# Pair scores as 512-column matmuls, ctx_low one step later, two first transfers from ScalarE

## The chip, the cores and the metric

The kernel runs on one core of one Trainium2 chip. The metric is device microseconds of one execution. TensorE does the matmuls and its weight loads, VectorE, ScalarE and GpSimd (POOL in the profile) work element by element, and SyncE (SP) issues DMAs. The engines run side by side and wait for each other by semaphores.

## The reference

Input x is 8 batches of 1024 rows of 1024; every batch has a context of 64 rows of 1024 and a mask. All is float32.

```
s   = layernorm(x) @ ctx.T / 32, masked         # 64 scores a row
x1  = x + softmax(s) @ ctx                      # the readout
y   = layernorm(x1)
out = x1 + y @ weight.T                         # base: 1024 columns
         + sum over the top 2 of 8 experts of
           gate * (y @ lora_A.T) @ lora_B.T * 2   # rank 16 each
```

The router's logits are y @ router_w.T; the gates are their softmax over the two largest.

## The kernel before, in words

The 8192 rows are 64 tiles of 128 rows. A tile is (b, j), batch b and j from 0 to 7. To keep float32 accuracy at the rate of the type float32r, each operand is split into a high part (rounded) and a low part (what is left), and a product is two or three matmuls: for the base product hi by hi, hi by lo and lo by hi (`three`, L1086 to L1088). The high part is made on ScalarE, the low part by a subtraction on VectorE.

Every engine runs its own list of steps, one per tile, written out by hand (`step` in each block; a hardware loop runs over batches 1 to 6). There is no planner: the order in a step is the order in which an engine takes its work. The opening, which handles tiles (0,0) and (0,1) and part of the next, has a list of its own.

TensorE's step for tile j: the base product of this tile for column group 0 (388 columns; the router's logits and the low-rank product are in it), then group 1 (386); in an odd step the scores of the pair of tiles j+3 and j+4 (`pair_scores`, L1105); the readout of tile j+2 (L1150, L1151: four matmuls of 512 columns with eT as the stationary operand); group 2; and the second low-rank product (`lora_second`), whose stationary operand is hT_hi and hT_lo.

Scores are computed turned. The stationary operand is a 128x128 block of ctxT: 64 columns with the high part of the centred context and 64 with its low part. The moving operand is a chunk of x of two tiles, 256 columns, first xT_hi (L1113) and then xT_lo (L1114). The eight chunks of the contraction make 16 matmuls that add up in the left half of the bank s_ps, 128 rows by 256 columns. VectorE turns them by 32x32 blocks (`s_transposes`, L860) into sq, four DMAs of SP carry sq's four groups of 32 rows to s_raw (`s_exchange`, L416), and `softmax_scores` (L822, L826, L830) adds the high and the low part of the context and takes the maximum.

VectorE's step, in order: `softmax_split` and `e_transposes` of tile j+2; one `xT_low`; `router_top`, which waits for the logits; `router_gate` and `h_transposes`; ctx_centre in step 4, the mask in step 5; `x2_transposes` of j+1; `s_transposes` in an odd step; `add_readout` and `norm2_stats` of j+2; `hT_low`; `norm2_moments` of j+2; `ctx_low` of the next batch in step 5 (L341 within the helper of that name, 1024 elements); `x2T_low` of j+1; ctx_sum_chunks in step 3, ctxT_low in step 4; `softmax_scores` of j+3; and the three adds of the base product.

The readout hangs on a long chain: moments on VectorE, rstd (L487) and shift (L490) on POOL, xn (L599) on ScalarE, then on SP's queue four issues of `exchange` (L374, xn to xq) and four of `e_exchange` (L410, the softmax's exponentials), and eT (L580) on ScalarE. SP's step also has the store, `h_exchange` (L404), the loads of x, xT and, in step 1, of the next batch's context, and `s_exchange` at the end of an even step.

In the opening, `pair_scores` is run for (0,2) and for (0,4). ScalarE converts xT of (0,6) as soon as the matmuls of (0,4) have read xT_hi, and then makes xn of (0,3). The matmul stream of the steady loop begins with step (0,2).

Scratch tiles such as sq and s_raw lie in w_raw[0], behind the part of it that holds a tile of x.

Of the kernel before, what the change touches and what calls it, by code (L numbers as in the profile page):

```python
# [23 lines left out]
def xattn_lora_moe_kernel(  # L24
# [35 lines left out]
    Q = 4  # L60
# [44 lines left out]
    with stack:  # L105
# [34 lines left out]
        xT_hi = sb("xT_hi", [P, 2, C, P], f32r)  # L140
        xT_lo = sb("xT_lo", [P, 2, C, P], f32r)
# [50 lines left out]
        sq = w_raw[0][:, C - 2, 0:T2]  # L192
        s_raw = w_raw[0][:, C - 3, 0:T2].rearrange("p (i k c) -> p i k c", i=Q, k=2)
# [122 lines left out]
        e_loaded = sem("e_loaded")  # L316
        sq_done = sem("sq_done")
# [16 lines left out]
        def first_ctx_low(engine, i, done):  # L334
            engine.wait_ge(ctx_hi_done, 1)
            engine.tensor_tensor(half(ctx_lo, i), half(ctx_raw, i), half(ctx_hi, i).bitcast(f32),
                                 ALU.subtract).then_inc(done, 1)

# [6 lines left out]
        def _(sp):  # L345
# [66 lines left out]
            def s_exchange(tile):  # L412

                sp.wait_ge(sq_done, pairs(tile, 1, 1 - 2))
                for i in range(Q):
                    sp.dma_start(s_raw[:, i].rearrange("p k c -> p (k c)"),  # L416
                                 sq[i * QP:(i + 1) * QP, :]).then_inc(s_loaded, 16)

            def step(tile, first=False):
# [19 lines left out]
                if j % 2 == 0 and exists(after(tile, 4)):  # L439
                    s_exchange(after(tile, 4))  # L440
# [84 lines left out]
        def _(act):  # L525
# [206 lines left out]
            norm1_squares((0, 4))  # L732
            for i in range(2):
                xT_high((0, 6), i)
# [10 lines left out]
        def _(dve):  # L745
# [112 lines left out]
            def s_transposes(tile):  # L858
                dve.wait_ge(sT_done, pairs(tile, 1, 1))
                dve.transpose(sq.rearrange("p (j k c) -> p k j c", k=2, c=QP),  # L860
                              s_ps[:, 0:T2].rearrange("p (k j c) -> p k j c", k=2, c=QP)).then_inc(sq_done, 1)
# [111 lines left out]
            def step(tile):  # L973
# [7 lines left out]
                if j % 2 == 1 and exists(after(tile, 3)):  # L981
                    xT_low(after(tile, 3), 1)
                router_top(tile)
# [17 lines left out]
                if j == TPB - 3 and exists((b, TPB)):  # L1001
                    ctx_low(dve, b + 1)
# [79 lines left out]
        def _(pe):  # L1082
# [23 lines left out]
            def pair_scores(tile):  # L1106
# [5 lines left out]
                for c in range(C):  # L1112
                    pe.matmul(s_ps[:, 0:T2], ctxT[:, c, :], xT_hi[:, :, c, :], start=(c == 0), stop=False)  # L1113
# [86 lines left out]
            def step(tile):  # L1200
# [6 lines left out]
                if j % 2 == 1 and exists(after(tile, 3)):  # L1207
                    pe.wait_ge(sq_done, pairs(after(tile, 3), 1, -2))
# [36 lines left out]
            pair_scores((0, 2))  # L1245
# [98 lines left out]
```

## Time and profile before

| | |
|---|---|
| time, median of 3 runs | 1054.68 us (1054.35 to 1054.8) |
| time of the profiled execution | 1054.39 us |
| its span | 1052.3 us |
| mean granted clock of TensorE over the span | 1.00 |
| busy: TensorE matmuls | 1043.5 us, 99% |
| busy: weight loads (beside the matmuls) | 1028.7 us, 98% |
| busy: VectorE | 817.3 us, 78% |
| busy: ScalarE | 477.7 us, 45% |
| busy: GpSimd | 147.8 us, 14% |

The span is the time from the first to the last recorded instruction of the profiled execution; the time has some 2 us around it. Busy time is the union of an engine's instructions. Matmuls are pipelined: one begins before the record of the one ahead has ended, so the rate of a stream is read from start to start and not from the durations. A granted clock of 1.00 is the upper of TensorE's two levels, 2.4 GHz.

### The profile page before, as it was taken

The page shows a single profiled execution, that of the slowest core. Times are in us where ns is not written, and L with a number is a line of the kernel's source. Part 1 is how long each engine was busy: PE and PEld are TensorE (multiplying, and loading weights), DVE is VectorE, ACT ScalarE, POOL GpSimd, SP SyncE. Part 2 cuts the span into 40 slices and gives each one's busy share as a digit, 9 for nine tenths or more (in the row PEclk, how much of TensorE's full clock was granted, in tenths as well). Part 3 has the DMA queues.
Part 4 walks back from the last instruction along what each step waited for, and adds up shares of the span by engine and source line. Part 5 has one row for each costly group of instructions (what it writes and reads, how often), then busy time and mean ns, then how long its engine had stood idle before and what let it go on. Part 6 is the DMA issues. An engine that isn't in the chain of part 4 may idle for free.

```text
span 1052.3 us, 18830 instructions
## 1 busy us (share of the span) xinstructions
PE 1043.5 (99%) x6078; PEld 1028.7 (98%) x6078; DVE 817.3 (78%) x2203; ACT 477.7 (45%) x929; POOL 147.8 (14%) x278
## 2 busy tenths in 40 slices
PE   8999999999999999999999999999999999999998
PEld 7999999999999999999999999999999999999998
DVE  6987887788777887878877888778888778777663
ACT  7754544445434544444444345344444444443320
POOL 3211211111111111111111111111111111111100
PEclk9999999999999999999999999999999999999999
DMA  8555556654556555475545655455654565554431
GB/s 306 201 160 124 149 154 163 170 147 122 149 158 179 143 123 142 143 201 131 152 115 150 185 149 150 135 132 171 163 150 137 118 174 153 152 149 114 114 75 58
DMA packets 157248, 156.81 MB, mean 149 GB/s; under 512 B 95120, under 2 KB 130064, under 8 KB 157200
## 3 DMA queue, kind: packets, MB, share of 16 engines
q1 hardware_dynamic: 156336, 154.82, 53.9%
q10 hardware_dynamic: 864, 1.45, 0.4%
q8 instruction: 18, 0.29, 0.1%
q14 instruction: 30, 0.25, 0.1%
HBM read 78.74 MB, written 33.55 MB: 107 GB/s over the span
## 4 chain that ended last, share of the span: by engine, by line
PE 95%; DVE 2%; DMA 1%; POOL 0%; issue 0%; ACT 0%; SPq 0%; ACTq 0%; DVEq 0%; POOLq 0%
PE base_ps L1086 28%; PE base_ps L1088 28%; PE base_ps L1087 28%; PE ro_ps L1150 3%; PE s_ps L1114 3%; PE ro_ps L1151 3%; PE s_ps L1113 3%; DMA xT_raw<-in_xT 1%; DVE stats L885 0%; DVE w_lo L331 0%; DVE x_first L879 0%; SPq L374 0%; DVE xT_lo L801 0%; DMA w_raw<-w_raw 0%; SPq L410 0%
## 5 line engine op out<-in xcount | busy, mean ns | idle before, releaser
L1086 PE MATMUL base_ps<-w_hi,xT_hi 128*128 128x388 f32 x1512 | 513.7, 340 | 0.0
L1088 PE MATMUL base_ps<-w_hi,xT_lo 128*128 128x388 f32 x1512 | 512.5, 339 | 0.0
L1087 PE MATMUL base_ps<-w_lo,xT_hi 128*128 128x388 f32 x1512 | 511.4, 338 | 0.0
L1087 PEld LDWEIGHTS base_ps<-w_lo,xT_hi 128*128 128x128 f32 x1512 | 284.7, 188 | 2.8
L1086 PEld LDWEIGHTS base_ps<-w_hi,xT_hi 128*128 128x128 f32 x1512 | 284.0, 188 | 2.7
L1088 PEld LDWEIGHTS base_ps<-w_hi,xT_lo 128*128 128x128 f32 x1512 | 284.3, 188 | 0.0
L487 POOL TENSOR_TENSOR rstd<-var_eps,neg_half 128x1 f32<-128x1 f32 x64 | 65.3, 1020 | 567.7 <-DVE var_eps L892 567.7
L901 DVE STREAM_TRANSPOSE x2T<-xq 128x512 f32<-128x512 f32 x122 | 121.5, 1072 | 5.3 <-DMA xq<-xn 4.7
L605 ACT CAST xT_hi<-x2T 128x512 fp32r<-128x512 f32 x122 | 69.6, 618 | 85.3 <-DVE x2T L901 85.3
L916 DVE MAX8 top<-base_ps 128x8 f32<-128x8 f32 x64 | 11.2, 174 | 106.8 <-PE base_ps L1088 106.8
L599 ACT ACTIVATE xn<-w_raw,shift,rstd 128x1024 f32<-128x1024 f32 x32 | 39.9, 1245 | 94.1 <-POOL shift L490 94.1
L908 DVE TENSOR_TENSOR xT_lo<-x2T,xT_hi 128x512 fp32r<-128x512 f32 x122 | 78.3, 683 | 0.0
L599 ACT ACTIVATE xn<-x_first,shift,rstd 128x1024 f32<-128x1024 f32 x29 | 36.1, 1245 | 82.7 <-POOL shift L490 82.7
L801 DVE TENSOR_TENSOR xT_lo<-xT_raw,xT_hi 128x1024 fp32r<-128x1024 f32 x62 | 73.4, 1185 | 0.0
L580 ACT CAST eT<-w_raw 128x128 fp32r<-128x128 f32 x60 | 17.9, 298 | 113.1 <-DMA w_raw<-w_raw 113.1
L609 ACT ACTIVATE gate_num<-top 128x1 f32<-128x1 f32 x64 | 18.9, 296 | 101.7 <-DVE top L916 101.7
L563 ACT CAST xT_hi<-xT_raw 128x1024 fp32r<-128x1024 f32 x64 | 63.9, 1045 | 1.5 <-PE s_ps L1114 1.4
L1086 PE MATMUL base_ps<-b_hi,hT_hi 128*128 128x386 f32 (+1 forms) x192 | 61.5, 320 | 0.0
L1088 PE MATMUL base_ps<-b_hi,hT_lo 128*128 128x386 f32 (+1 forms) x192 | 61.0, 318 | 0.0
L1087 PE MATMUL base_ps<-b_lo,hT_hi 128*128 128x386 f32 (+1 forms) x192 | 60.9, 317 | 0.0
L1114 PE MATMUL s_ps<-xT_lo,ctxT 128*128 128x256 f32 x248 | 60.6, 283 | 0.0
L1113 PE MATMUL s_ps<-xT_hi,ctxT 128*128 128x256 f32 x248 | 60.3, 279 | 0.0
(128 smaller groups left out, 1382.5 us busy)
## 6 DMA issues: line engine op xcount, KB each, us to landing
xT_raw<-in_xT SPq DMA_DIRECT2D x62, 512.0 KB, 5.3
xq<-xn SPq DMA_DIRECT2D x244, 128.0 KB, 3.6
w_raw<-in_x SPq DMA_DIRECT2D x32, 512.0 KB, 3.5
out<-x_first SPq DMA_DIRECT2D x32, 512.0 KB, 2.7
out<-w_raw SPq DMA_DIRECT2D x31, 512.0 KB, 2.7
x_first<-in_x SPq DMA_DIRECT2D x30, 512.0 KB, 3.5
h<-w_raw SPq DMA_DIRECT2D x248, 16.0 KB, 1.9
w_raw<-w_raw SPq DMA_DIRECT2D x120, 32.0 KB, 1.9
```

Of the source, the lines that this page charges most:

```text
L487: pool.tensor_tensor(rstd2[:, :], var_eps2[:, :], neg_half[:, :], ALU.pow).then_inc(rstd2_done, 1)
L563: act.copy(xT_hi[:, i], xT_raw[:, k, i]).then_inc(xT_hi_done, 1)
L599: act.activation(xn[:, :], x(tile), ACT.Identity, bias=shift2[:, :], scale=rstd2[:, :]).then_inc(xn_done, 1)
L605: act.copy(chunks(xT2_hi[:, tile[1] % 2], i), chunks(x2T, i)).then_inc(x2T_hi_done, 1)
L801: dve.tensor_tensor(xT_lo[:, i], xT_raw[:, tile[1] // 2 % 2, i], xT_hi[:, i].bitcast(f32), ALU.subtract).then_inc(xT_split, 1)
L901: dve.transpose(out_[:, i * QS:(i + 1) * QS], xq[:, i * QS:(i + 1) * QS, :].rearrange("p g (c n) -> p g c n", n=QP)).then_inc(x2T_done, 1)
L908: dve.tensor_tensor(chunks(xT2_lo[:, k], i), chunks(x2T, i), chunks(xT2_hi[:, k], i).bitcast(f32), ALU.subtract).then_inc(x2T_split, 1)
L1086: pe.matmul(out_, a_hi, w_h, start=start, stop=False, skip_group_check=again)
L1087: pe.matmul(out_, a_hi, w_l, start=False, stop=False, skip_group_check=again)
L1088: return pe.matmul(out_, a_lo, w_h, start=False, stop=stop, skip_group_check=again)
L1113: pe.matmul(s_ps[:, 0:T2], ctxT[:, c, :], xT_hi[:, :, c, :], start=(c == 0), stop=False)
L1114: mm = pe.matmul(s_ps[:, 0:T2], ctxT[:, c, :], xT_lo[:, :, c, :], start=False, stop=(c == C - 1))
```

## The change

The scores of a pair are computed by 8 matmuls of 512 columns, in place of 16 of 256. xT_hi and xT_lo become the two halves of one tile, xT_parts, so that a moving operand can take a chunk of both; the products with the high and the low part of x land in the left and the right half of s_ps. VectorE adds the halves (`tensor_reduce` into s_sum, in PSUM the two terms lie 256 columns apart) and then transposes s_sum, behind a semaphore of its own. TensorE's wait before the next pair is for that sum instead of for the transposes. The pair (0,2) keeps the old form under the name first_pair_scores.

ctx_low of the next batch moves from step 5, between the moments and x2T_low, to step 6, in front of router_top. Of the four transfers of the scores of the pair (0,4), the first two are issued by ScalarE, between the squares of (0,4) and the conversion of xT of (0,6); it waits there for sq_done.

```diff
--- before.py
+++ after.py
@@ -137,8 +137,9 @@
         xn = sb("xn", [P, D])
         xq = sb("xq", [P, Q, DQ])
         xT_raw = sb("xT_raw", [P, 2, 2, C, P])
-        xT_hi = sb("xT_hi", [P, 2, C, P], f32r)
-        xT_lo = sb("xT_lo", [P, 2, C, P], f32r)
+        xT_parts = sb("xT_parts", [P, 2, 2, C, P], f32r)
+        xT_hi = xT_parts[:, 0]
+        xT_lo = xT_parts[:, 1]
         sT = sb("sT", [P, T2])
         x2T = sb("x2T", [P, C, P])
         xT2_hi = sb("xT2_hi", [P, 2, C, P], f32r)
@@ -190,6 +191,7 @@
         eq = w_raw[0][:, C - 1, P:2 * P]
         e_raw = w_raw[0][:, C - 1, 2 * P:3 * P]
         sq = w_raw[0][:, C - 2, 0:T2]
+        s_sum = w_raw[0][:, C - 4, 0:T2]
         s_raw = w_raw[0][:, C - 3, 0:T2].rearrange("p (i k c) -> p i k c", i=Q, k=2)
 
 
@@ -314,6 +316,7 @@
         hq_done = sem("hq_done")
         eq_done = sem("eq_done")
         e_loaded = sem("e_loaded")
+        s_sum_done = sem("s_sum_done")
         sq_done = sem("sq_done")
         s_loaded = sem("s_loaded")
         h_loaded = sem("h_loaded")
@@ -335,6 +338,13 @@
             engine.wait_ge(ctx_hi_done, 1)
             engine.tensor_tensor(half(ctx_lo, i), half(ctx_raw, i), half(ctx_hi, i).bitcast(f32),
                                  ALU.subtract).then_inc(done, 1)
+
+        def s_exchange(engine, tile, parts):
+
+            engine.wait_ge(sq_done, pairs(tile, 1, 1 - 2))
+            for i in parts:
+                engine.dma_start(s_raw[:, i].rearrange("p k c -> p (k c)"),
+                                 sq[i * QP:(i + 1) * QP, :]).then_inc(s_loaded, 16)
 
         def ctx_low(engine, b):
             engine.wait_ge(ctx_hi_done, b + 1)
@@ -409,13 +419,6 @@
                 for i in range(Q):
                     sp.dma_start(e_raw[:, i * QP:(i + 1) * QP], eq[i * QP:(i + 1) * QP, :]).then_inc(e_loaded, 16)
 
-            def s_exchange(tile):
-
-                sp.wait_ge(sq_done, pairs(tile, 1, 1 - 2))
-                for i in range(Q):
-                    sp.dma_start(s_raw[:, i].rearrange("p k c -> p (k c)"),
-                                 sq[i * QP:(i + 1) * QP, :]).then_inc(s_loaded, 16)
-
             def step(tile, first=False):
 
                 b, j = tile
@@ -437,7 +440,7 @@
                     sp.wait_ge(xT_split, pairs((0, 2), 2, 2))
                     load_xT((0, 6))
                 if j % 2 == 0 and exists(after(tile, 4)):
-                    s_exchange(after(tile, 4))
+                    s_exchange(sp, after(tile, 4), range(2 if first else 0, Q))
                 if j % 2 == 1 and exists(after(tile, 7)):
                     sp.wait_ge(xT_split, pairs(after(tile, 3), 2, 2))
                     load_xT(after(tile, 7))
@@ -730,6 +733,7 @@
             first_eT_copy((0, 3))
             norm1_mean((0, 4))
             norm1_squares((0, 4))
+            s_exchange(act, (0, 4), range(2))
             for i in range(2):
                 xT_high((0, 6), i)
             norm2((0, 3))
@@ -857,8 +861,11 @@
 
             def s_transposes(tile):
                 dve.wait_ge(sT_done, pairs(tile, 1, 1))
+                dve.tensor_reduce(out=s_sum, in_=s_ps[:, :].rearrange("p (l t) -> p t l", l=2), axis=AX.X,
+                                  op=ALU.add).then_inc(s_sum_done, 1)
+                dve.wait_ge(s_sum_done, pairs(tile, 1, 1 - 2))
                 dve.transpose(sq.rearrange("p (j k c) -> p k j c", k=2, c=QP),
-                              s_ps[:, 0:T2].rearrange("p (k j c) -> p k j c", k=2, c=QP)).then_inc(sq_done, 1)
+                              s_sum.rearrange("p (k j c) -> p k j c", k=2, c=QP)).then_inc(sq_done, 1)
 
             def first_softmax_split(tile):
                 dve.wait_ge(exp_done, count(tile, 2, 2))
@@ -980,6 +987,8 @@
                     xT_low(after(tile, 4), 0)
                 if j % 2 == 1 and exists(after(tile, 3)):
                     xT_low(after(tile, 3), 1)
+                if j == TPB - 2 and exists((b, TPB)):
+                    ctx_low(dve, b + 1)
                 router_top(tile)
                 router_gate(tile)
                 h_transposes(tile)
@@ -998,8 +1007,6 @@
                 hT_low(tile)
                 if exists(nxt2):
                     norm2_moments(nxt2)
-                if j == TPB - 3 and exists((b, TPB)):
-                    ctx_low(dve, b + 1)
                 if exists(nxt):
                     x2T_low(nxt)
                 if j == TPB - 5 and exists((b, TPB)):
@@ -1110,6 +1117,13 @@
                     pe.wait_ge(ctxT_split, b + j // TPB + 1)
                 pe.wait_ge(xT_split, pairs(tile, 2, 2))
                 for c in range(C):
+                    mm = pe.matmul(s_ps[:, 0:2 * T2], ctxT[:, c, :], xT_parts[:, :, :, c, :], start=(c == 0), stop=(c == C - 1))
+                mm.then_inc(sT_done, 1)
+
+            def first_pair_scores(tile):
+
+                pe.wait_ge(xT_split, pairs(tile, 2, 2))
+                for c in range(C):
                     pe.matmul(s_ps[:, 0:T2], ctxT[:, c, :], xT_hi[:, :, c, :], start=(c == 0), stop=False)
                     mm = pe.matmul(s_ps[:, 0:T2], ctxT[:, c, :], xT_lo[:, :, c, :], start=False, stop=(c == C - 1))
                 mm.then_inc(sT_done, 1)
@@ -1205,7 +1219,7 @@
                     ctx_mean(b + 1)
                 base(tile, 1, range(C))
                 if j % 2 == 1 and exists(after(tile, 3)):
-                    pe.wait_ge(sq_done, pairs(after(tile, 3), 1, -2))
+                    pe.wait_ge(s_sum_done, pairs(after(tile, 3), 1, -2))
                     pair_scores(after(tile, 3))
                 if exists(nxt2):
                     readout(nxt2)
@@ -1242,7 +1256,7 @@
             first_base(2, 0, range(C))
             first_x2_transposes((0, 1))
             first_base(2, 1, range(C))
-            pair_scores((0, 2))
+            first_pair_scores((0, 2))
             base((0, 1), 0, range(2))
             scores((0, 2))
             base((0, 1), 0, range(2, 6))
```

## Rows read from the trace of the kernel before

**Rows 1.** The page, section 1: busy us, share, instructions.

```profile
PE 1043.5 (99%) x6078; PEld 1028.7 (98%) x6078; DVE 817.3 (78%) x2203; ACT 477.7 (45%) x929; POOL 147.8 (14%) x278
```

**Rows 2.** Waits: engine, tile, line, releaser; total us, times, longest.

```profile
DVE top L916 <- PE base_ps L1088: 106.8, 61, 3.8
...
PE ro_ps L1150 <- ACT eT L580: 0.9, 1, 0.9
```

**Rows 3.** Timeline, TensorE, step (0,3): start, us, line, operation.

```profile
84.56 0.28 PE L1113 MATMUL s_ps<-xT_hi,ctxT 128*128 128x256 f32 x1
...
86.47 0.39 PE L1150 MATMUL ro_ps<-ctx_hi,eT 128*128 128x512 f32 x1
...
87.40 0.33 PE L1086 MATMUL base_ps<-w_hi,xT_hi 128*128 128x386 f32 x1
```

**Rows 4.** Lines by form, VectorE: busy us, mean ns, idle before.

```profile
L908 DVE TENSOR_TENSOR xT_lo<-x2T,xT_hi 128x512 fp32r<-128x512 f32 x122 | 78.3, 683 | 0.0
...
L947 DVE SCALAR_TENSOR_TENSOR h<-base_ps,gate_inv,w_dense 128x128 f32<-128x128 f32 x62 | 21.8, 351 | 2.2
...
L830 DVE TENSOR_REDUCE neg_max<-s_all 128x1 f32<-128x64 f32 x60 | 13.2, 220 | 2.1
...
L762 DVE TENSOR_REDUCE ctx_sum<-ctxT_raw 128x64 f32<-128x512 f32 x8 | 8.6, 1078 | 3.7 <-DMA ctxT_raw<-in_ctxT 3.7
...
L940 DVE SCALAR_TENSOR_TENSOR h<-base_ps,gate_inv,w_dense 128x64 f32<-128x64 f32 x4 | 1.0, 330 | 0.1
```

**Rows 5.** Timeline, steps (3,5) and (3,6), VectorE and weight loads.

```profile
503.65 0.45 DVE L860 STREAM_TRANSPOSE w_raw<-s_ps 128x256 f32<-128x256 f32 x1 [1.47 <-PE s_ps L1114]
...
506.83 0.28 DVE L955 TENSOR_TENSOR hT_lo<-h,hT_hi 128x128 fp32r<-128x128 f32 x1
...
507.44 1.22 DVE L341 TENSOR_TENSOR ctx_lo<-ctx_raw,ctx_hi 128x1024 fp32r<-128x1024 f32 x1
...
508.46 0.19 PEld L1086 LDWEIGHTS base_ps<-b_hi,hT_hi 128*128 128x128 f32 x1
...
514.60 0.17 DVE L916 MAX8 top<-base_ps 128x8 f32<-128x8 f32 x1 [0.98 <-PE base_ps L1088]
```

**Rows 6.** Timeline, POOL, behind the moments of steps (3,1) and (3,5).

```profile
443.32 0.99 POOL L487 TENSOR_TENSOR rstd<-var_eps,neg_half 128x1 f32<-128x1 f32 x1 [10.46 <-DVE var_eps L892]
...
507.54 1.52 POOL L487 TENSOR_TENSOR rstd<-var_eps,neg_half 128x1 f32<-128x1 f32 x1 [10.05 <-DVE var_eps L892]
509.20 0.70 POOL L490 TENSOR_TENSOR shift<-neg_mean,rstd 128x1 f32<-128x1 f32 x1
```

**Rows 7.** Timeline, eT and its readout, steps (3,2), (3,6) and (5,0).

```profile
452.63 0.30 ACT L580 CAST eT<-w_raw 128x128 fp32r<-128x128 f32 x1 [1.74 <-DMA w_raw<-w_raw]
...
454.29 0.39 PE L1150 MATMUL ro_ps<-ctx_hi,eT 128*128 128x512 f32 x1
...
517.64 0.30 ACT L580 CAST eT<-w_raw 128x128 fp32r<-128x128 f32 x1 [2.53 <-DMA w_raw<-w_raw]
...
518.51 0.39 PE L1150 MATMUL ro_ps<-ctx_hi,eT 128*128 128x512 f32 x1
...
677.86 0.30 ACT L580 CAST eT<-w_raw 128x128 fp32r<-128x128 f32 x1 [2.56 <-DMA w_raw<-w_raw]
...
678.71 0.39 PE L1150 MATMUL ro_ps<-ctx_hi,eT 128*128 128x512 f32 x1
```

**Rows 8.** Timeline, the opening: a ScalarE issue, and the first steady readout's chain.

```profile
1.19 0.46 ACTq L677 DMA_DIRECT2D xT_raw<-in_xT  x1
...
58.17 0.45 DVE L860 STREAM_TRANSPOSE w_raw<-s_ps 128x256 f32<-128x256 f32 x1 [0.89 <-PE s_ps L1114]
...
58.23 2.00 ACT L563 CAST xT_hi<-xT_raw 128x1024 fp32r<-128x1024 f32 x2 [1.37 <-PE s_ps L1114]
61.33 1.24 ACT L599 ACTIVATE xn<-x_first,shift,rstd 128x1024 f32<-128x1024 f32 x1 [1.10 <-POOL shift L490]
...
69.41 0.50 PE L1150 MATMUL ro_ps<-ctx_hi,eT 128*128 128x512 f32 x1 [0.88 <-ACT eT L580]
```

## The prediction

> **What bounds the kernel now.** I read the page's busy line first [rows 1]: TensorE is busy 1043.5 of 1052.3 us, its weight loads 1028.7 beside that; VectorE has 817.3, ScalarE less than half. Then the table of waits [rows 2]: in the whole span TensorE has one wait for another engine after the opening, 0.9 us for eT at the first readout of the steady loop. VectorE, on the other hand, waits 106.8 us in 61 places for the router's logits (1.75 us a tile), and for nothing else as much. So from 70 us to the end the matmul stream alone sets the time: an edit pays if it shortens that stream, and costs only if it makes TensorE wait. Last I read the timeline of one odd step and one even step, to measure each margin by which something arrives before TensorE wants it, and the timeline of 56 to 70 us, where there is no margin.
>
> Matmuls overlap in the records, so I count start to start, never the duration.
>
> **1. 512-column scores (TensorE).** The 16 matmuls of 256 columns of a pair start at 84.56 and the readout behind them at 86.47, so they take 1.91 us; read in the same way, all 31 pairs have a mean of 1.906, or 0.1191 a matmul [rows 3]. A 512-column float32r matmul is in the same rows: the four of a readout take 87.40 - 86.47 = 0.93; all 60 of the steady loop have a mean of 0.923, so 0.231 each. Eight of these make 1.845 us: 0.061 less per pair. The pair of tiles (0,2) keeps its old form, (0,0) another one, so 30 pairs change: 30 x 0.061 = 1.83 us gained. The columns are the same 4096 either way; only what each matmul costs beyond its columns is saved. The new right side is four runs of 128 columns where the readout's is one run. Bounds: at least what two old ones cost, 0.238, if the seams cost as much as now (gain 0); at most 0.2133 for the bare columns at the 2.4 GHz that the trace grants (gain 8 x 0.025 x 30 = 6.0). I take the readout's row, the only one at 512 columns.
>
> The Trainium skill (TensorE: Matmul & The Clock Gate, Back-to-back issue gap) gives a fixed 2.5 ns beyond the columns of each isolated matmul. By it eight saved matmuls would give 20 ns a pair, 0.6 us in all, which speaks against the change; the trace has 12 ns beyond 256 columns and 17 beyond 512, so it does not agree, and gives three times the gain.
>
> **2. The extra sum (VectorE).** 30 times a TENSOR_REDUCE of 512 elements in PSUM to 256, in pairs 256 apart, with the transposes waiting for it. Not in the trace. Lower bound: one element at a time without a penalty for steps, as the 512-element subtraction, 0.683 us [rows 4]. The nearest row is the reduce of ctx_sum, also 512 elements read with a step: 1.078. That steps cost is seen elsewhere: 64 stepped elements (L940) take 0.330, 128 plain ones (L947) 0.351. Upper bound: if the price lies in results instead of in elements, neg_max (64 elements, one result, 0.220) and the subtraction's rate put 6 ns on each of ctx_sum's 64 results, and 256 results make 2.25 us. I take 1.10, by the nearest row, with 0.03 for the hand-over: everything behind it in an odd step slips by up to 1.13 us.
>
> What is behind it, in VectorE's order: readout sums, statistics of tile+2, hT_low, moments, x2T_low, softmax, the adds. VectorE sat idle before the transposes, so nothing absorbs the slip ahead. (a) hT_low ends at 507.11; TensorE loads hT_hi at 508.46 [rows 5]: 1.35 of room, 0.22 left. (b) moments, POOL's rstd, xn, SP's four xq issues and four e issues, eT, readout of the next even step: eT is ready at 452.93 and wanted at 454.29, 1.36 of room, 0.23 left in most steps 0 and 2 of a batch; but where transfers were late, as at 678.16 against 678.71, 0.55, some 0.6 is lost [rows 7]. Of the 15 such steps three have less than 1.13 of room (0.98, 0.71 and 0.55); with the lot of the transfers drawn anew I take 0.3 us in all. (c) The next router waits 1.75 us on average, and takes up the rest [rows 2].
>
> **3. ctx_low one step later.** 1.22 us leave step 5 and stand before the router of step 6 [rows 5], where VectorE sat 0.98 us idle [rows 5]. In step 5 it cancels the slip of x2T_low, whose room there was smallest; in step 6 the router comes 0.1 to 0.4 late, and its followers have more room than that. It also frees POOL: its rstd takes 1.52 us in step 5 and 0.99 in step 1 [rows 6], and the product behind it 0.70. So xn of step 5 comes at least 0.53 earlier (0.9, if that product falls to 0.3 as well), and the 0.57 us between eT (517.94) and its readout (518.51) [rows 7] becomes 0.57 + 0.9 - 1.13 = 0.34, or -0.03 at worst. Value to the sum: nothing in either direction, seven times; without the move, step 6 would lose 7 x 0.6 = 4 us. ctx_lo is wanted only by the readout in that same step, four us after it is made. SP's next context load waits for ctx_split, but in the next batch.
>
> The Trainium skill (SBUF — State Buffer, Who interferes with whom) says a VectorE operation with both inputs in SBUF blocks a GpSimd one that reads SBUF for its whole length. The row agrees with it: rstd ends when ctx_low's 1.22 us are nearly over. The sum would not change by it.
>
> **4. The opening.** The stall of rows 8 is fed by this chain: s_transposes 58.17, statistics, POOL, xn at 61.33, four xq issues, four e issues, landing, eT, readout at 69.41, 0.88 idle. The extra sum is in it: +1.13. And ScalarE now waits for the transposes before it may convert xT(0,6): it was at 58.23, and becomes 58.62 + 1.13 = 59.75, then two DMA issues at 0.46 each [rows 8], then 2.00 us of conversion: xn can start at about 62.7, 1.4 later than 61.33, whereas VectorE's chain alone would give 1.07 (with the pair's 0.06 back). So the first readout comes 1.4 us later. The two parts sent by ScalarE bring the first softmax scores some 1.3 us earlier than four issues on SP would, but e_transposes need not be earlier than SP's release from the xq issues, so that buys nothing here. Bounds: +0.6 (reduce 0.683, cheap issues) to +2.6 (reduce 2.25). Everything later is relative to TensorE and gets room from the stall.
>
> **Sum.** -1.83 + 1.4 + 0.3 = -0.1 us. The profiled execution took 1054.39 (span 1052.3 and 2.1 around it), so 1054.3; the median shown is 0.3 above that execution, so 1054.6. What this kernel's measurement can tell from no change is about 0.2%, 2.1 us: under 1052.6 is faster, over 1056.8 slower.
>
> **Rivals.**
> A, the reduce is cheap (0.7 us) and the issues hide: the opening costs 0.6, no later readout is late: -1.83 + 0.6 = -1.2, 1053.5. For it: the plain rate of 0.683; against it: ctx_sum's row.
> B, four runs cost what the old seams cost: the stream gains nothing, 1054.68 + 1.4 + 0.3 = 1056.4. For it: the lo matmuls start 0.123 before the next, the hi ones 0.116, so something other than columns is paid. Against it: the readouts of rows 3. By the skill's fixed cost above (TensorE: Matmul & The Clock Gate), the gain of 0.6 us would make it 1055.8, which this case's range covers.
> C, the other side: hT_low becomes late. It decides once the reduce passes about 1.3 us (room 1.35 for hT). At 2.25 it is 2.28 - 1.35 = 0.93 in each of 29 odd steps, 27 us, and the opening and the stream 2.6 - 1.8: 1083; at 1.6 us it is 29 x 0.28 = 8: 1063. For it: a price per result can't be excluded by rows 4. Against it: L940 against L947, where the number of results can't be it.
> D, the stream gains more: at the bare columns, 6.0 us and 1054.68 - 6.0 + 1.7 = 1050.4; it is faster than the bound from 0.222 a matmul on. For it: the eight score matmuls share each weight block and write one bank. Against it: no 512-column matmul of this trace starts so close to the next.
>
> **How the numbers follow.** Forecast 0.52, A 0.22, B 0.10, C 0.08, D 0.08. The predicted time is the forecast's. Its own spread is about 1 us. The range goes from 1052.4 (A with the old stall gone too, 1053.5 - 0.9) to 1056.8 (B with a few more late readouts); it leaves out D and C, 16 in 100. Faster by over 0.2%: D and a third of A's low end, 0.15. Slower: C and a part of B, 0.12. Same: 0.73.
>
> **What would show it.** Right: 8 score matmuls in each odd step, their starts 0.23 apart; a reduce of 1.1 us; no waits of TensorE for hT; a first readout at about 70.8 with over 2 us idle before it; POOL's rstd at 0.99 in step 5; the router's wait on VectorE smaller in even steps. Wrong: a reduce under 0.8 or over 1.3; TensorE waiting for hT in odd steps or eT in many even ones; score starts off 0.23; the opening's stall at or under 1 us.

## The result, and the profile after

The kernel after takes 1056.13 us (median of 15 runs, 1054.33 to 1058.39), the kernel before 1054.39 (15 runs on the same chip, 1053.84 to 1056.69): 1.0016 times as long, interval 1.0008 to 1.0023. The forecast was 1054.6, no change. The time lies inside the range given, but the change is 1.7 us slower, beyond its interval, where -0.1 was forecast. The profiled execution took 1056.94 (span 1055.2 and 1.78 around it). Against [rows 1 and 2], the page's busy line and two waits:

```profile
PE 1045.3 (99%) x5838; PEld 1019.5 (97%) x5838; DVE 833.4 (79%) x2233; ACT 476.6 (45%) x929; POOL 144.2 (14%) x278
```

```profile
DVE top L923 <- PE base_ps L1095: 91.4, 61, 3.8
...
PE ro_ps L1164 <- ACT eT L583: 2.8, 2, 2.5
```

VectorE's wait for the router's logits went from 106.8 to 91.4 us: it took up most of the 20 us of new reduces. TensorE has 240 instructions fewer, and yet waits for eT not 0.9 us once but 2.8 in two places. No wait of it for hT is listed. The pair of step (0,3), against [rows 3]:

```profile
88.01 2.03 PE L1120 MATMUL s_ps<-xT_parts,ctxT 128*128 128x512 f32 x8
89.87 0.39 PE L1164 MATMUL ro_ps<-ctx_hi,eT 128*128 128x512 f32 x1
```

From start to start that is 1.86 us; over the 30 changed pairs 1.863, so 0.233 a matmul, where 1.845 and 0.231 were taken. And the new reduce beside ctx_sum's in the lines by form of VectorE (mean ns behind the comma), against [rows 4]:

```profile
L864 DVE TENSOR_REDUCE w_raw<-s_ps 128x256 f32<-128x512 f32 x30 | 20.7, 689 | 43.0 <-PE s_ps L1120 43.0
```

It takes the subtraction's plain rate, 0.69 us, and not ctx_sum's 1.08. Next the opening, against [rows 8], from the timeline of 57 to 73 us:

```profile
57.94 2.02 PE L1120 MATMUL s_ps<-xT_parts,ctxT 128*128 128x512 f32 x8
...
59.99 0.69 DVE L864 TENSOR_REDUCE w_raw<-s_ps 128x256 f32<-128x512 f32 x1 [0.84 <-PE s_ps L1120]
...
60.72 0.45 DVE L867 STREAM_TRANSPOSE w_raw<-w_raw 128x256 f32<-128x256 f32 x1
...
61.19 1.31 SPq L346 DMA_DIRECT2D w_raw<-w_raw  x2
61.20 1.57 ACTq L346 DMA_DIRECT2D w_raw<-w_raw  x2
...
62.87 2.00 ACT L566 CAST xT_parts<-xT_raw 128x1024 fp32r<-128x1024 f32 x2 [4.14 <-issue]
...
64.78 1.24 ACT L602 ACTIVATE xn<-x_first,shift,rstd 128x1024 f32<-128x1024 f32 x1
...
72.50 0.30 ACT L583 CAST eT<-w_raw 128x128 fp32r<-128x128 f32 x1 [3.41 <-DMA w_raw<-w_raw]
...
72.84 0.50 PE L1164 MATMUL ro_ps<-ctx_hi,eT 128*128 128x512 f32 x1 [2.49 <-ACT eT L583]
```

The chain is the predicted one: reduce, transposes, ScalarE's two issues, its 2.00 us of conversion, xn, eT, readout. But the reduce takes 0.69 and not 1.10, ScalarE's issues take 1.57 us for two and not 0.92, and TensorE idles 2.49 instead of 0.88: the stall grew by 1.6 us.

Here everything also stands 1.86 us later than before on the clock of the span (the pair (0,2) starts at 37.21 instead of 35.35), by something that happened ahead of any edited line. The windows of this profile (window, its length, busy time by engine, granted clock, DMA share, GB/s) and the wait that came first:

```profile
10.00:12.00 2.00, 0.63 (x3) 0.63 (x4) 0.52 (x3) 2.00 (x4) 0.60 (x2) 0.64 1.03 363
12.00:16.00 4.00, 4.00 (x20) 4.00 (x19) 3.33 (x9) 3.47 (x9) 1.53 (x3) 0.50 1.06 384
16.00:18.00 2.00, 2.00 (x10) 1.62 (x10) 1.14 (x2) 2.00 (x4) 1.75 (x1) 0.65 1.06 376
...
72.00:74.00 2.00, 1.16 (x5) 0.97 (x6) 2.00 (x3) 0.49 (x2) 0.00 (x0) 1.00 0.81 280
```

```profile
11.37 0.48 PE L1238 MATMUL ro_ps<-ident,sT 128*128 128x128 f32 x1 [1.61 <-ACT sT L626]
```

TensorE sat idle 1.61 us for the first tile's scores (the first load of x landed 0.85 later than in the profile before, where the same wait is 0.84 and the clock stays 1.00), and from 10.56 to 17.39 us the granted clock was at its 1.2 GHz level. Behind the longer wait of 2.49 us, at 72.84, it stayed at 1.00 in this execution (last line of the windows). A low clock is in runs of both kernels. What sets them apart is how often: every run lists its mean granted clock, and it is 0.998 or less ("under 1.00" from here on) in 13 of the 15 runs of after. In three later series of 33 runs each, the kernel before has that in 4, 4 and 3. A run's mean does not say where in the kernel the clock was low. The two runs of after that kept 1.00 took 1054.33 and 1055.35; the 13 others have a median of 1056.17.

### The profile page after: what moved, and what is told of

It is laid out like the page before. It is cut to its first block, busy times and chain, and to the rows that moved or that the text cites. A ratio compares the mean times of both kernels' runs of the same rounds, so it can differ in the third digit from the quotient of the medians.

```text
span 1055.2 us, 18380 instructions
## 1 busy us (share of the span) xinstructions
PE 1045.3 (99%) x5838; PEld 1019.5 (97%) x5838; DVE 833.4 (79%) x2233; ACT 476.6 (45%) x929; POOL 144.2 (14%) x278
## 3 DMA queue, kind: packets, MB, share of 16 engines
q10 hardware_dynamic: 1152, 1.52, 0.4%
## 4 chain that ended last, share of the span: by engine, by line
PE 94%; DVE 2%; DMA 1%; SPq 1%; issue 1%; POOL 1%; ACT 0%; ACTq 0%; DVEq 0%; POOLq 0%
PE base_ps L1093 27%; PE base_ps L1095 27%; PE base_ps L1094 27%; PE s_ps L1120 5%; PE ro_ps L1164 3%; PE ro_ps L1165 3%; DMA xT_raw<-in_xT 1%; SPq L420 0%; SPq L384 0%; DVE stats L892 0%; PE base_ps L1142 0%; DMA w_raw<-w_raw 0%; DVE w_lo L334 0%; DVE x_first L886 0%; ACT xn L602 0%
## 5 line engine op out<-in xcount | busy, mean ns | idle before, releaser
L490 POOL TENSOR_TENSOR rstd<-var_eps,neg_half 128x1 f32<-128x1 f32 x64 | 61.5, 960 | 573.7 <-DVE var_eps L899 573.7
L923 DVE MAX8 top<-base_ps 128x8 f32<-128x8 f32 x64 | 11.1, 174 | 91.4 <-PE base_ps L1095 91.4
L805 DVE TENSOR_TENSOR xT_parts<-xT_raw,xT_parts 128x1024 fp32r<-128x1024 f32 x62 | 73.4, 1185 | 0.0
L566 ACT CAST xT_parts<-xT_raw 128x1024 fp32r<-128x1024 f32 x64 | 63.9, 1045 | 4.1 <-issue 4.1
L1120 PE MATMUL s_ps<-xT_parts,ctxT 128*128 128x512 f32 x240 | 60.8, 395 | 0.0
L484 POOL TENSOR_TENSOR var_eps<-sum_sq,eps_sum 128x1 f32<-128x1 f32 x64 | 16.8, 262 | 279.2 <-ACT x2T L557 278.2
```

The source lines that it names most:

```text
L490: pool.tensor_tensor(rstd2[:, :], var_eps2[:, :], neg_half[:, :], ALU.pow).then_inc(rstd2_done, 1)
L566: act.copy(xT_hi[:, i], xT_raw[:, k, i]).then_inc(xT_hi_done, 1)
L805: dve.tensor_tensor(xT_lo[:, i], xT_raw[:, tile[1] // 2 % 2, i], xT_hi[:, i].bitcast(f32), ALU.subtract).then_inc(xT_split, 1)
L1120: mm = pe.matmul(s_ps[:, 0:2 * T2], ctxT[:, c, :], xT_parts[:, :, :, c, :], start=(c == 0), stop=(c == C - 1))
```

## The experiments

Kernels were run 11 times each beside 33 runs of the kernel before (medians 1054.36, 1054.21 and 1054.31 in the three series); "clock under 1.00 in k" counts runs. Of each kernel one execution was profiled, so a figure from a timeline is of that one execution, and can differ from the median by some tenths of a us. Lines left out of an edit are marked by "...".

**1. The wide scores and the sum alone.** ctx_low back in step 5, all transfers on SP:

```diff
-                    s_exchange(sp, after(tile, 4), range(2 if first else 0, Q))
+                    s_exchange(sp, after(tile, 4), range(Q))
...
-            s_exchange(act, (0, 4), range(2))
...
-                if j == TPB - 2 and exists((b, TPB)):
-                    ctx_low(dve, b + 1)
                 router_top(tile)
...
                     norm2_moments(nxt2)
+                if j == TPB - 3 and exists((b, TPB)):
+                    ctx_low(dve, b + 1)
```

> The 512-column scores and the extra sum alone: ctx_low stays in step 5, all four first transfers stay on SP. Theory: the stream gives 30 x 0.041 = 1.2 us back, the opening's stall grows by the sum alone (0.72 less 0.04), and in step 6 of each batch the readout's eT comes 0.69 later with 0.57 of room, up to 0.15 lost seven times: together 0 to 0.5 us less to 0.5 us more than before where the granted clock stays 1.00 over the span, and 1.7 us more for each 3.4 us at the lower level. Rival (the extra sum or the moving operand's form itself slows the loop): over 1 us more at clock 1.00.

1056.11 us (1055.39 to 1057.53), 1.0018 [1.0009, 1.0027], clock under 1.00 in 1. A miss: slower by 1.75 with the clock intact. Its timeline at the moments of step (3,5) and the readout of (3,6):

```profile
508.87 1.52 POOL L490 TENSOR_TENSOR rstd<-var_eps,neg_half 128x1 f32<-128x1 f32 x1 [10.52 <-DVE var_eps L898]
...
510.53 0.70 POOL L493 TENSOR_TENSOR shift<-neg_mean,rstd 128x1 f32<-128x1 f32 x1
...
518.97 0.30 ACT L583 CAST eT<-w_raw 128x128 fp32r<-128x128 f32 x1 [3.06 <-DMA w_raw<-w_raw]
...
519.33 0.50 PE L1163 MATMUL ro_ps<-ctx_hi,eT 128*128 128x512 f32 x1
```

and the same places in the kernel after, with ctx_low moved:

```profile
511.37 0.99 POOL L490 TENSOR_TENSOR rstd<-var_eps,neg_half 128x1 f32<-128x1 f32 x1 [10.53 <-DVE var_eps L899]
...
512.50 0.30 POOL L493 TENSOR_TENSOR shift<-neg_mean,rstd 128x1 f32<-128x1 f32 x1
...
516.42 1.22 DVE L351 TENSOR_TENSOR ctx_lo<-ctx_raw,ctx_hi 128x1024 fp32r<-128x1024 f32 x1
...
520.56 0.30 ACT L583 CAST eT<-w_raw 128x128 fp32r<-128x128 f32 x1 [2.14 <-DMA w_raw<-w_raw]
...
521.83 0.39 PE L1164 MATMUL ro_ps<-ctx_hi,eT 128*128 128x512 f32 x1
```

Without the move eT is ready at 519.27 and the readout starts 0.06 behind it: no room. From one step to the next TensorE takes 15.14 to 15.19 instead of 15.03 us there, in each of batches 1 to 6: 0.9 lost in all. In batch 0 the step takes 16.01 (before: 15.17), and step 4 of batch 7 takes 15.27 instead of 15.03. With the move there is 0.97 of room [rows 7: 0.57] and batches 1 to 6 lose nothing. So the move does what it says, POOL's 1.52 and 0.70 become 0.99 and 0.30; its worth is the difference to experiment 2, the same kernel with the move, which is 1.1 us by the medians. The profiled execution took 1055.40, 1.0 over before: 0.7 more of stall, 1.3 less of stream, 0.9, 0.8 and 0.2 of late readouts, and a start that happened to be 0.4 quicker. The median is 0.7 above that execution; this part stays open.

**2. After, with all four first transfers on SP.**

```diff
-            s_exchange(act, (0, 4), range(2))
...
-                    s_exchange(sp, after(tile, 4), range(2 if first else 0, Q))
+                    s_exchange(sp, after(tile, 4), range(Q))
```

> The changed kernel with all four first transfers on SP, so ScalarE neither waits for the transposes nor issues. Theory: the first readout of the loop comes 0.7 us after that of before instead of 1.5, so 0.8 us less than the changed kernel at the same granted clock, and about 0.5 less than before at clock 1.00. Rival (the softmax's side of the chain then becomes late, because four issues on SP land 1.3 us later): no gain over the changed kernel.

1055.01 (1054.11 to 1056.57), 1.0006 [0.9997, 1.0015], clock under 1.00 in 4: 1.1 under after, where the theory had 0.8 at the same clock, but not the 0.5 under before that it forecast at full clock. The first steady readout:

```profile
69.42 0.50 PE L1163 MATMUL ro_ps<-ctx_hi,eT 128*128 128x512 f32 x1 [1.58 <-ACT eT L583]
```

The wait is 1.58, 0.7 over before: that much is the reduce's, and the 0.9 up to 2.49 is the two issues on ScalarE.

**3. ScalarE's two transfers alone, on the kernel before.**

```diff
-                    s_exchange(after(tile, 4))
+                    s_exchange(sp, after(tile, 4), range(2 if first else 0, Q))
...
+            s_exchange(act, (0, 4), range(2))
             for i in range(2):
                 xT_high((0, 6), i)
```

> The kernel before with nothing but the two first transfers moved to ScalarE. Theory: ScalarE's wait and its two issues (1.6 us in the changed kernel's trace) push the conversion of xT(0,6) and so xn(0,3), and the idle time before the first readout of the loop goes from 0.9 to 1.8 us or a little more: 0.9 to 1.0 us slower at clock 1.00, and in some runs the clock falls behind that idle time and 1.7 us come on top. Rival (the transfers are free, or help the softmax's side): no change within 0.3 us.

1054.73 (1054.38 to 1057.14), 1.0009 [1.0000, 1.0018], clock under 1.00 in 3. The three lines of its opening:

```profile
58.23 1.58 ACTq L343 DMA_DIRECT2D w_raw<-w_raw  x2
...
59.91 2.00 ACT L563 CAST xT_hi<-xT_raw 128x1024 fp32r<-128x1024 f32 x2 [3.48 <-issue]
...
69.89 0.50 PE L1151 MATMUL ro_ps<-ctx_hi,eT 128*128 128x512 f32 x1 [1.76 <-ACT eT L580]
```

1.58 us for two issues again, the conversion at 59.91 instead of 58.23, and the wait 1.76 for 0.88. By themselves they bring nothing and cost 0.9 in the opening; the median is 0.5 over before, less than the 0.9 to 1.0 of the theory, since it also has 0.3 less time outside the span (1.78 instead of 2.1).

**4. and 5. Filling the wait at 10 us.** Eight idle matmuls behind the first scores, in the kernel after and in the kernel before:

```diff
             first_scores(0)
+            warm(8)
```

> The changed kernel with eight more 128-column matmuls into an unused bank between the first scores and the wait for their copy, where TensorE sat idle 1.6 us before the clock fell. Theory (the fall of the clock in the opening is 1.7 us of the loss, and comes of that idle stretch): clock 1.00 in nearly all runs, and 1.5 us less than the changed kernel in the median. Rival (the clock falls for a reason that these do not touch, or the loss is in the loop): clock 0.998 as often as now, no gain.

> The kernel before with the same eight matmuls: the control for the one above. Theory: the clock was mostly 1.00 without them, so the median changes by less than 0.5 us, and the few runs of 1055 us and over go. Then the warmed pair shows the change alone: the changed kernel 0.3 us slower than before to 0.5 faster. Rival: as much gained as in the changed kernel.

After so filled: 1056.17 (1054.42 to 1057.36), 1.0012 [1.0003, 1.0021], clock under 1.00 still in 6; those six have a median of 1056.55, the five others 1055.17. Before so filled: 1055.67 (1054.97 to 1056.49), 1.0010 [1.0001, 1.0019], under 1.00 in none; the filling itself costs 1.3, where under 0.5 was expected. (Each of these idle matmuls shows as two in the timeline, 16 here.) So the theory that the fall at 10 us is all of it was wrong. The profile of the filled kernel after shows the second place, in the timeline of TensorE and in the windows:

```profile
71.15 0.50 PE L1164 MATMUL ro_ps<-ctx_hi,eT 128*128 128x512 f32 x1 [2.48 <-ACT eT L583]
...
72.19 0.39 PE L1093 MATMUL base_ps<-w_hi,xT_hi 128*128 128x386 f32 x1
72.37 0.53 PE L1094 MATMUL base_ps<-w_lo,xT_hi 128*128 128x386 f32 x1
72.69 0.53 PE L1095 MATMUL base_ps<-w_hi,xT_lo 128*128 128x386 f32 x1
```

```profile
72.00:74.00 2.00, 2.00 (x9) 1.95 (x8) 1.97 (x4) 1.14 (x2) 0.00 (x0) 0.59 0.22 33
74.00:76.00 2.00, 2.00 (x8) 2.00 (x7) 1.97 (x8) 0.30 (x1) 0.66 (x1) 0.56 1.07 299
76.00:80.00 4.00, 4.00 (x26) 4.00 (x25) 2.61 (x7) 3.16 (x7) 0.63 (x2) 1.00 0.94 373
```

The wait of 2.48 us ends at 71.15, and 1.2 us behind it, at 72.35, the clock falls, for 3.4 us. The base matmuls start 0.32 apart instead of 0.18, and the stretch from readout to readout takes 18.55 instead of 17.03: 1.5 us, on top of the wait itself. In the profile of after the same wait has no such fall behind it: it comes in some executions and not in others.

**6. Filling the wait at 70 us.** 14 idle matmuls ahead of the first steady readout of the kernel after:

```diff
+                if isinstance(b, int) and tile == (0, 2):
+                    pe.wait_ge(out_done, FREE + G + 1)
+                    warm(14)
                 if exists(nxt2):
                     readout(nxt2)
```

> The changed kernel with 14 matmuls of 128 columns into an unused bank in front of TensorE's wait for the first readout of the loop, so that the 2.5 us there are not idle. They take about 1.5 us and end before eT is there. Theory (the clock falls behind this idle time): clock 1.00 in nearly all runs, median 1054.7, 1.4 us under the changed kernel, and what is left over before is the longer stall less the stream's gain. Rival (the clock falls elsewhere, by chance of the opening): clock 0.998 in as many runs as in the changed kernel, 12 to 13 of 15, and no gain.

1055.30 (1054.44 to 1056.53), 1.0009 [1.0000, 1.0018], clock under 1.00 in 1 instead of in 13 of 15: 0.83 under after. Its windows:

```profile
68.00:72.00 4.00, 4.00 (x34) 3.82 (x33) 2.62 (x5) 0.71 (x2) 0.00 (x0) 1.00 0.59 158
72.00:74.00 2.00, 2.00 (x13) 2.00 (x12) 1.97 (x4) 1.03 (x3) 0.00 (x0) 1.00 0.36 62
74.00:76.00 2.00, 2.00 (x13) 2.00 (x12) 1.97 (x7) 0.00 (x0) 0.85 (x1) 1.00 1.03 348
```

and its timeline:

```profile
67.93 3.29 PE L1142 MATMUL base_ps<-one_dth 128*128 128x128 f32 x28
...
70.23 0.30 ACT L583 CAST eT<-w_raw 128x128 fp32r<-128x128 f32 x1 [3.40 <-DMA w_raw<-w_raw]
...
70.97 0.48 PE L1164 MATMUL ro_ps<-ctx_hi,eT 128*128 128x512 f32 x1
```

The same stall, with TensorE kept at work in it, is followed by no loss of clock, and nothing ahead of it was edited: so most of after's low clocks have to come behind this wait. The filling was not free, as its text expected. The 14 matmuls show as 28, take 3 us instead of 1.5 and outlast the wait: eT is ready at 70.53 and the readout starts 0.44 later, where it starts 0.05 behind eT in after. So 0.4 has to be added to the 0.83 that the edit gives back. Counted against each series' own runs of before, the 0.83 is 0.65. By this experiment the clock's part in the slowdown is thus 1.0 to 1.2 us.

**7. The first pair in its old form.** All transfers on SP, and the pair (0,4), which stands in the stall's chain, with its 16 matmuls of 256 columns and no sum:

```diff
-            s_transposes((0, 4))
+            first_s_transposes((0, 4))
...
             readout((0, 3))
-            pair_scores((0, 4))
+            first_pair_scores((0, 4))
```

> The changed kernel with all first transfers on SP and the pair (0,4) in the old form, without the sum: nothing of the opening's chain is changed any more, 29 pairs have the new form. Theory: idle time of 0.9 us before the first readout as before, 0.16 us gained in each batch of the loop, less one late readout in batch 0: 0.5 to 1.0 us faster than before. Rival (thin margins in even steps take it back): within 0.2 us of before.

1053.97 (1053.24 to 1056.67), 1.0000 [0.9991, 1.0009], clock under 1.00 in 1: 2.2 under after, but level with before, where 0.5 to 1.0 less was expected. The first wait is 0.9 again, as before. Two readouts of the loop came 0.6 late, one more than the theory had, and took back the stream's gain.

**8. The move of ctx_low alone, on the kernel before.**

```diff
+                if j == TPB - 2 and exists((b, TPB)):
+                    ctx_low(dve, b + 1)
                 router_top(tile)
...
-                if j == TPB - 3 and exists((b, TPB)):
-                    ctx_low(dve, b + 1)
```

> The kernel before with only ctx_low moved to step 6. Theory: no wait of TensorE hangs on it, so the time is that of before within 0.3 us; POOL's rstd in step 5 takes 0.99 us in place of 1.52, and eT of step 6 is ready about 1.4 us before its readout instead of 0.57. Rival (the router of step 6 comes late and someone waits for it): 0.5 us slower or more.

1054.14 (1053.7 to 1056.43), 0.9999 [0.9990, 1.0008], clock under 1.00 in 3: nothing by itself, and 1.5 us of room where the kernel before has 0.57. Its profiled execution is one of the 3. TensorE waited 0.92 us for the first tile's scores, hardly more than the 0.84 of the profile before, and the clock was low for 3.4 us from 10.36 on:

```profile
10.00:12.00 2.00, 1.46 (x7) 1.46 (x8) 0.55 (x2) 2.00 (x5) 1.24 (x3) 0.59 1.06 393
12.00:16.00 4.00, 4.00 (x25) 3.72 (x23) 3.53 (x10) 3.62 (x9) 1.72 (x2) 0.78 1.06 376
```

So a fall at 10 us needs no long wait and none of the edited matmuls.

**9. and 10. The matmuls without the sum, and the sum without the matmuls.** Both with all transfers on SP:

```diff
-                dve.tensor_reduce(out=s_sum, in_=s_ps[:, :].rearrange("p (l t) -> p t l", l=2), axis=AX.X,
-                                  op=ALU.add).then_inc(s_sum_done, 1)
```

```diff
-                dve.tensor_reduce(out=s_sum, in_=s_ps[:, :].rearrange("p (l t) -> p t l", l=2), axis=AX.X,
+                dve.tensor_reduce(out=s_sum, in_=s_ps[:, 0:T2].unsqueeze(2).to_broadcast([P, T2, 2]), axis=AX.X,
...
-                    mm = pe.matmul(s_ps[:, 0:2 * T2], ctxT[:, c, :], xT_parts[:, :, :, c, :], start=(c == 0), stop=(c == C - 1))
+                    pe.matmul(s_ps[:, 0:T2], ctxT[:, c, :], xT_hi[:, :, c, :], start=(c == 0), stop=False)
+                    mm = pe.matmul(s_ps[:, 0:T2], ctxT[:, c, :], xT_lo[:, :, c, :], start=False, stop=(c == C - 1))
```

> The changed kernel with all first transfers on SP and without the sum of the halves: only the products with the high part of x reach the scores, the low part is left out. It shows the stream's gain alone. Theory: idle time before the first readout 0.9 us as before, each pair 0.041 us shorter, room before even readouts as before: 1.1 to 1.2 us faster than before (1053.1), and 1.2 to 1.4 under the same kernel with the sum (e2_sp_transfers). Rival (the matmuls' form costs room elsewhere, the sum is harmless): as e2_sp_transfers, 1055.

> The changed kernel with all first transfers on SP, the old 16 matmuls of 256 columns, and a sum of the same shape that adds the left half of the bank to itself, so the scores are doubled. It shows the price of the sum alone. Theory: 0.7 us more idle time before the first readout and 0.5 us of late even readouts in the first batches: 1.2 us slower than before (1055.5). Rival: the sum is hidden, as before within 0.3.

Without the sum: 1053.04 (1052.7 to 1054.04), 0.9985 [0.9976, 0.9994], 1.3 faster than before, the size of the stream's gain. (In its profile the first wait is 1.05, 0.17 longer, and the one late readout of before is gone.) With the sum and the old matmuls: 1054.80 (1054.39 to 1057.55), 1.0005 [0.9996, 1.0014], where 0.7 of a longer first wait (1.6 us) explains the 0.5; the 0.5 of late readouts that made the theory's 1.2 are not in its profile. The reduce:

```profile
L863 DVE TENSOR_REDUCE w_raw<-s_ps 128x256 f32<-128x512 f32 x30 | 20.7, 690 | 47.1 <-PE s_ps L1120 47.1
```

It stood at 0.69 although it read the same half twice, without the step of 256. The two do not add up: the sum costs 2.0 us on the new matmuls (experiment 2 less the kernel without the sum) and 0.5 on the old. In the profiles it is 1.3 and 0.6: experiment 2 has two late readouts, 0.8 together, and the old matmuls none. Why they were late in the one and not in the other no run shows.

**11. and 12. A shorter chain.** xn of each tile in two halves, so that SP issues the first two of its four transfers while ScalarE makes the second half; in experiment 7's kernel, and in the kernel before:

```diff
-                act.activation(xn[:, :], x(tile), ACT.Identity, bias=shift2[:, :],
-                               scale=rstd2[:, :]).then_inc(xn_done, 1)
+                for i, done in enumerate([xn_half, xn_done]):
+                    act.activation(half(xn, i), half(x(tile), i), ACT.Identity, bias=shift2[:, :],
+                                   scale=rstd2[:, :]).then_inc(done, 1)
...
-                sp.wait_ge(xn_done, count(tile, 1, 1))
+                sp.wait_ge(xn_half, count(tile, 1, 1 - 3))
                 for a in range(Q):
+                    if a == 2:
+                        sp.wait_ge(xn_done, count(tile, 1, 1))
```

> e7_old_first_pair with xn written in two halves, SP's first two xq issues going after the first half. Theory (the room before even readouts is what the changed kernel lacks): eT comes about 0.6 us earlier in each step, so the late readouts of the loop go, and the idle time of 0.9 us before the first readout of the loop falls to about 0.4: 1.5 us faster than before, 1052.7. Rival (ScalarE's extra instruction or the transfers' contention takes it back): as e7_old_first_pair, 1054.0.

> The kernel before with the same halves, as the control. Theory: in its loop no readout is late, so only the opening's idle time shrinks: 0.4 to 0.6 us faster than before, 1053.7, and 1.0 us slower than e11_split_xn. Rival: nothing gained.

On the new scores: **1052.58** (1052.19 to 1053.28), 0.9980 [0.9971, 0.9989], faster than both kernels. On the old ones: 1053.72 (1053.39 to 1054.04), 0.9991 [0.9982, 1.0000]. From the timeline of the first:

```profile
60.88 1.52 ACT L606 ACTIVATE xn<-x_first,shift,rstd 128x512 f32<-128x512 f32 x2 [1.10 <-POOL shift L496]
...
61.72 2.58 SPq L387 DMA_DIRECT2D xq<-xn  x4
...
68.94 0.50 PE L1172 MATMUL ro_ps<-ctx_hi,eT 128*128 128x512 f32 x1 [0.84 <-ACT eT L586]
```

SP starts 0.84 after xn does, not 1.27. That gives the loop's eT its room back: one readout late by 0.04, where experiment 7 had two at 0.6, and the stream's 1.3 us stay. The opening's wait did not fall to 0.4 as expected: it is 0.84, for there the four e issues now wait for the softmax's transposes, done at 64.72, and not for the xq issues, done at 64.30:

```profile
64.42 0.30 DVE L863 STREAM_TRANSPOSE w_raw<-e_split 128x128 f32<-128x128 f32 x1
...
64.75 2.55 SPq L423 DMA_DIRECT2D w_raw<-w_raw  x4
```

Of the 1.7 us under before, the halves of xn bring 0.6 on the old kernel too (experiment 12), and 0.3 of that is time outside the span, 1.78 instead of 2.1, for which no cause was found. The new scores bring 1.1.

## Why the prediction went wrong

The forecast was -0.1 and the measured change +1.7 us. The terms that the sum priced come to +1.0 in the profile of after: the stream's was 0.6 too good (-1.3 for -1.83), the late readouts' 0.3 and the stall's 0.2 too low. A term that it did not have, the clock, adds the largest part, 1.0 to 1.3, and time outside the span takes 0.3 off.

**The step that failed** is the opening (part 4, and its line in the sum). It put the stall at its own length, and went on: "Everything later is relative to TensorE and gets room from the stall." The stall's mechanism and nearly its size were right (+1.4; measured +1.6), but behind a wait of 2.5 us TensorE's clock is also low in most runs: 13 of 15 under 1.00, against one in nine of the kernel before. The kernels ordered by their first wait for eT: at 2.5 us 13 of 15 and (experiment 4, its start filled) 6 of 11 runs under 1.00; at 1.6 to 1.8 (experiments 1, 2, 3, 10) 9 of 44; at 1.1 and less, before among them, 17 of 165; filled (6) 1 of 11. The filling is what shows the cause; the rest is only an order that agrees. The price lies between the 1.0 of experiment 6, as reckoned there, and the 1.3 between after's runs at 1.00 (1054.84, only two) and its others. In single unprofiled runs it is not known at which of the two places the clock fell, and in the one profiled run of after it fell at the first. The Trainium skill (TensorE: Matmul & The Clock Gate, HAM oscillation — how this bites in real kernels) says of a kernel with waits for data of some 3 to 5 us that they throttle TensorE again and that the loss is half of the throttled time. Experiment 4's rows have it behind a shorter wait, 2.48 us, with 3.4 us at the lower level and 1.5 lost, a little under half. The sum read the table of waits and never asked what each wait does to the matmuls behind it.

**Part 1, the stream:** the mechanism held, the size not: 0.233 a matmul for 0.231, so 0.042 a pair and 1.3 us in all for 1.83. The four runs of 128 columns cost some 2 ns more than the readout's single run. Experiment 9 measured it by time, -1.3. Rivals B (nothing) and D (0.213) fell.

**Part 2, the sum:** 0.69 for 1.10. Of the two rows it lay between, the far one was right, and the prediction's own sign of being wrong, a reduce under 0.8, came. Experiment 10 shows that the step of 256 in PSUM costs nothing (690 ns without it, 689 with it); why ctx_sum's 512 elements cost 1.08 from SBUF no run shows. No wait for hT is listed, and rival C fell with it. Rival A named this price, and did not come, since its second half (issues that hide) was wrong.

**Part 2 (b), late readouts:** +0.3 was the term, +0.6 came in the profile, but not as reckoned. The reduce was cheap, and most steps 0 and 2 kept 0.8 to 0.9 of room instead of 0.23. Two readouts were late all the same. One in step 6 of batch 0:

```profile
129.40 2.55 SPq L384 DMA_DIRECT2D xq<-xn  x4
131.99 3.86 SPq L420 DMA_DIRECT2D w_raw<-w_raw  x4
...
137.15 0.30 ACT L583 CAST eT<-w_raw 128x128 fp32r<-128x128 f32 x1 [3.08 <-DMA w_raw<-w_raw]
...
137.59 0.47 PE L1164 MATMUL ro_ps<-ctx_hi,eT 128*128 128x512 f32 x1 [0.31 <-ACT eT L583]
```

Four issues that take 2.54 in the opening (from 68.66 on) take 3.86 here: one of them took 1.9 us. This step took 15.60 us instead of 15.03 (before: 15.17). In step 4 of batch 7 four xq issues took 3.57, and the step 15.24 instead of 15.03 (before: 15.03). Single issues of over 1.1 us on SP are in each profile looked at, 5 in before's and 9 in after's; they cost only where the room is under a microsecond.

**Part 3, ctx_low:** right in every instruction (0.99 and 0.30 on POOL, 1.22 in front of the router, no loss). It does save something: 1.1 us between experiments 1 and 2, against 4 with the reduce at 1.10. One reading was off: in [rows 5 and 6] rstd ends at 509.06, 0.40 behind the end of ctx_low (508.66) and not ahead of it. And its 0.99 us is not its time alone. In the opening of after it takes 0.55, beside an add that reads PSUM; at 0.99 it starts beside x2T_low, a subtraction of 0.68 us with both operands in SBUF, and at 1.52 beside ctx_low's 1.22.

**Part 4's parts:** the reduce gave +0.7 (1.13 taken), ScalarE's two issues +0.9 (0.3 beyond VectorE's chain). Both errors are of one size and cancelled; that the stall's term came out near was luck. Had only the reduce's price been right, the sum would have been lower, and further off. The issue's row [rows 8: 0.46] was a load from HBM; these copy from SBUF to SBUF and take 0.8 each.

The account: stall +1.6, stream -1.3, late readouts +0.6, together +1.0 (profile of after); with -0.3 outside the span (medians) +0.7. The two runs of after at full clock are 0.45 over before. The ten runs of experiment 6 at full clock are 1.0 over, 0.4 of it the filling. The clock adds 1.0 to 1.3, so 1.7 to 2.0 in all, against 1.7 measured.

**Left open:** the 0.3 less outside the span (2.1 before and in most experiments; 1.78 wherever ScalarE has the two transfers, but also in 11 and 12, which do not); 0.7 of experiment 1; why the sum costs more on the new matmuls than on the old; what makes the clock fall in one execution and not in the next behind the same wait.

## What to carry to other kernels

A wait of TensorE, where it sets the time, can have two prices: its own length, and what the clock does to the work behind it. Before an edit lengthens the one wait that such a kernel still has, look at the granted clock behind the longest waits of the trace, and shorten the chain that feeds it first: here the old first pair and xn in halves made a loss of 1.7 us into a gain of 1.7. Merging two matmuls saved 5 ns here, so it paid only once nothing that it added stood in a chain with under a microsecond of room; and a price for an issue has to come from a row with the same kind of source and the same engine.

## What the runs showed of the hardware

- In one execution TensorE's granted clock fell to its lower level 1.2 us behind an idle stretch of 2.48 us in an otherwise full stream, and stayed there for 3.4 us; in another it stayed at 1.00 behind 2.49 us. With that stretch filled it was under 1.00 in 1 of 11 runs, unfilled in 13 of 15.
- At the start of the kernel it fell within an idle stretch of 1.61 us, for 6.8 us, and within one of 0.92, for 3.4 us; with one of 0.84 it did not.
- TENSOR_REDUCE of 512 fp32 elements in pairs took 689 ns from PSUM with 256 results; ctx_sum, also 512 elements, takes 1078 from SBUF with 64 results.
- A DMA issue took 0.79 us on ScalarE's queue and 0.65 on SP's for the same SBUF-to-SBUF parts; a single such issue on SP took up to 1.9.
- POOL's rstd (128 x 1) took 0.55 us in the opening, 0.99 beside a VectorE subtraction of 0.68 us from SBUF, and 1.52 beside one of 1.22 us.
- A float32r matmul of 512 columns in four runs of 128 started 0.233 us after the one before, in one run 0.231.
